# A fused decoder block on one core: reciprocal halves behind the copy of P, and the second weights ahead of the residual

## The chip, the core and the metric

The kernel runs on one core of one Trainium2 chip. The metric is the device time of one execution in microseconds (us). A run of the kernel gives one such time; the median of three runs is compared.

## What is computed

The program takes 4096 tokens of 512 features (16 sequences of 256) and runs four stages over them. Cut to what matters here:

```python
x = layernorm(x + mamba_and_gated_mlp(x))               # stages 1 and 2, untouched by the change
# stage 3, attention: 16 heads of 32, over 256 context tokens per sequence
q, k, v = x @ Wq.T + bq, ctx @ Wk.T + bk, ctx @ Wv.T + bv
p = softmax(q k^T / sqrt(32))                            # per head
x = layernorm(x + (p v) @ Wo.T + bo)
# stage 4, quantised MLP: 512 -> 2048 -> 512, the second product in 8 bits
h  = relu(x @ w1.T + b1);  hq = fp8(h);  wq = fp8(w2)
x  = layernorm(x + fp16(hq @ wq.T + b2))
```

## The kernel before

The tokens are cut into 8 tiles of 512 (NP = 8), that is two sequences each. Every stage is one function that writes five queues, one per engine, and a stage runs all 8 tiles before the next begins: tile 0 and tile 7 are written out, tiles 1 to 6 are a hardware loop (`steps`, line 60). The order of work on each engine is the order in which the code issues it; engines meet only at semaphores (`wait_ge`). Products in 32 bits are made from three products of rounded parts, high and low (`mm3`, lines 75 to 77), so each operand needs a "high" copy by ACT and a "low" rest by DVE or POOL.

**Attention** (`stage_attention`). A tile is 8 steps, n = 0 to 7; a step is four heads of one sequence. In step n the names stand for this:

- `scores(i, n + 1)` (L1701, PE): the scores of the next step into four banks SC.
- `row_max` (L1567, DVE): the negative maximum of each row, before ACT's exponentials (`exp`, L1417), which also leave the row sums in `sums`.
- `turn_p` (L1710, PE): four transposes of one head's P into the single bank PT; `take_pT` (L1573, DVE) copies PT to `at_pT`. There is one PT bank, so each `turn_p` waits for the copy before it (`pte`).
- `values` (L1722, PE): P times V for the step before, which needs all four copies of that step.
- `project(i, slot, half)` (L75 to L77, PE): two half projections for each of 16 slots, put between these as filling. Their results go alternately to banks AB[0] (even slots) and AB[1] (odd slots); DVE takes them in `take` (L1543, L1547 or L1553), which counts `pout`.
- `invert(i, g)`, at odd n, when the four heads' sums of both sequences are there: DVE's reciprocal (L1578), then its high half (the CAST, L1580) and its low half (L1582) into `at_r_hl`. `turn_r` (L1730, PE) transposes these into AB[1] at the next even n, ACT copies them (`take_rT`, L1423), `spread` (L1735) broadcasts them, and `normalise` (L1587, DVE) scales the heads' output.
- `statistics` (L1557) and `gather` (L1563), DVE: the layer norm's statistics of the tile before, in steps 3, 4 and 5. POOL then makes the reciprocal root (L889, L891) and normalises (L1498), SP stores the tile (L1366), and loads the next residual into the same tile of memory, to which POOL adds the bias (L1521). POOL also makes the low halves of the context (L1346) and of the heads' output (L1503).

DVE's queue in an odd step n of the loop:

```python
take_pT(i, n, 0); take_pT(i, n, 1)
split_u(i + 1, ...)                 # n = 1 and 3
statistics / gather                 # n = 3, (4), 5
invert(i, n // 2)
take_pT(i, n, 2)
take(i, 2 * n + 1)
row_max(i, n + 1, 0) ...
```

**Quantised MLP** (`stage_quantised_mlp`). Per tile PE makes 16 chunks of the hidden layer (`chunk`, 12 matmuls each), ACT turns each into 8 bits (`relu`, L1970), and then PE makes four groups of 16 matmuls with the 8-bit second weights `w2q` (L2071). The first 7 chunks of tile 0 are made in the last attention tile. The weights come through 8 staging tiles `qm_stage`: 16 pieces of w1, then 16 pieces of w2 (256 KB each), each of which waits for its staging tile's last user. ACT rounds each w2 piece to 8 bits (L214) between its relus of tile 0. SP's single queue issues all of it, in the order of the code: 8 pieces of w2, the store of attention's last tile (L1366), the tokens of tile 1 (L1933), the residual of tile 0 (L1937), 8 more pieces of w2.

## Time and profile before

| | us |
|---|---|
| median of 3 runs (lowest, highest) | 2758.64 (2756.23, 2761.95) |
| the profiled execution, its own time | 2757.51 |
| its span, first to last instruction | 2755.7 |
| PE busy | 2675.0 (97%) |
| DVE busy | 1530.9 (56%) |
| ACT busy | 1021.6 (37%) |
| POOL busy | 670.6 (24%) |

The span is what the trace covers; 1.8 us of the execution lie outside it. In the span the mixer ends at about 780 us, the gated MLP at about 1590, attention runs from about 1592 to 2285, the quantised MLP from there to the end. A middle tile of attention takes 84.43 us, the distance between two equal instructions of neighbouring tiles (a transposition at 1783.27 us and its like at 1867.70).

### The profile page before, as it was taken

The page shows a single profiled execution, that of the slowest core. Times are in us where ns is not written, and L with a number is a line of the kernel's source. Part 1 is how long each engine was busy: PE and PEld are TensorE (multiplying, and loading weights), DVE is VectorE, ACT ScalarE, POOL GpSimd, SP SyncE. Part 2 cuts the span into 40 slices and gives each one's busy share as a digit, 9 for nine tenths or more (in the row PEclk, how much of TensorE's full clock was granted, in tenths as well). Part 3 has the DMA queues.
Part 4 walks back from the last instruction along what each step waited for, and adds up shares of the span by engine and source line. Part 5 has one row for each costly group of instructions (what it writes and reads, how often), then busy time and mean ns, then how long its engine had stood idle before and what let it go on. Part 6 is the DMA issues. An engine that isn't in the chain of part 4 may idle for free.

```text
span 2755.7 us, 42318 instructions
## 1 busy us (share of the span) xinstructions
PE 2675.0 (97%) x15264; PEld 2074.0 (75%) x15264; DVE 1530.9 (56%) x2561; ACT 1021.6 (37%) x2375; POOL 670.6 (24%) x594
## 2 busy tenths in 40 slices
PE   7999999999999999999999989999999998999999
PEld 5777777777778888888888867777777766777776
DVE  8797797788785331333133377777777773111122
ACT  6334334434434222122212255555555553222221
POOL 5553453463361100010001101332223321000000
PEclk9999999999999999999999999999999999999999
DMA  4101101101114101110112030111011123211111
GB/s 152 46 2 46 46 0 46 46 0 46 46 47 139 62 19 42 61 61 14 47 61 96 23 108 11 60 61 39 30 61 53 57 93 114 83 48 46 46 46 46
DMA packets 85482, 147.83 MB, mean 54 GB/s; under 512 B 4032, under 2 KB 17984, under 8 KB 85408
## 3 DMA queue, kind: packets, MB, share of 16 engines
q1 hardware_dynamic: 85408, 146.84, 15.3%
q8 instruction: 46, 0.75, 0.1%
q14 instruction: 28, 0.23, 0.0%
HBM read 113.27 MB, written 33.55 MB: 53 GB/s over the span
## 4 chain that ended last, share of the span: by engine, by line
PE 87%; DVE 8%; issue 2%; ACT 1%; DMA 1%; POOL 0%; DVEq 0%; SPq 0%; POOLq 0%; ACTq 0%
PE ps L75 22%; PE ps L77 22%; PE ps L76 22%; PE ps L1710 4%; PE ps L2071 4%; PE ps L780 3%; PE ps L1722 2%; DVE mx_cv L585 1%; PE ps L1701 1%; PE ps L756 1%; DVE at_pT L1573 1%; DVE mx_m L593 1%; PE ps L768 1%; PE ps L1730 1%; DVE at_r_hl L1580 1%
## 5 line engine op out<-in xcount | busy, mean ns | idle before, releaser
L1417 ACT ACTIVATE at_pr<-ps,at_nm 128x256 f32<-128x256 f32 x512 | 235.9, 473 | 191.7 <-DVE at_nm L1567 191.7
L1110 DVE TENSOR_TENSOR gm_m_lo<-gm_m,gm_m_hi 128x512 fp32r<-128x512 f32 (+1 forms) x88 | 61.0, 693 | 416.8 <-ACT gm_m_hi L1027 416.8
L75 PE MATMUL ps<-sh_u_hi,gm_gu_hi 128*128 128x512 f32 (+1 forms) x704 | 274.7, 390 | 1.6 <-DVE gm_gu_lo L227 1.6
L76 PE MATMUL ps<-sh_u_lo,gm_gu_hi 128*128 128x512 f32 (+1 forms) x704 | 274.6, 390 | 0.0
L77 PE MATMUL ps<-sh_u_hi,gm_gu_lo 128*128 128x512 f32 (+1 forms) x704 | 274.6, 390 | 0.0
L1573 DVE COPY at_pT<-ps 128x512 f32<-128x512 f32 x256 | 176.1, 688 | 127.4 <-PE ps L1710 124.1
L1021 ACT ACTIVATE gm_sg<-ps 128x512 f32<-128x512 f32 (+1 forms) x88 | 52.7, 598 | 518.4 <-PE ps L77 518.3
L75 PE MATMUL ps<-sh_u_hi,qm_w_hi 128*128 128x512 f32 x512 | 201.4, 393 | 0.0
L77 PE MATMUL ps<-sh_u_hi,qm_w_lo 128*128 128x512 f32 x512 | 199.4, 390 | 0.0
L76 PE MATMUL ps<-sh_u_lo,qm_w_hi 128*128 128x512 f32 x512 | 199.3, 389 | 0.0
L530 POOL TENSOR_TENSOR mx_m<-mx_m,mx_g 128x512 f32<-128x512 f32 x128 | 185.0, 1445 | 45.6 <-DVE mx_m L595 45.3
L585 DVE SCALAR_TENSOR_TENSOR mx_cv<-ps,mx_cols,mx_cv 128x510 f32<-128x510 f32 (+2 forms) x240 | 176.2, 742 | 23.3 <-ACT mx_cv L427 16.7
L1710 PE MATMUL ps<-sh_ident,at_pr 128*128 128x128 f32 x1024 | 160.8, 280 | 28.3 <-DVE at_pT L1573 26.6
L1970 ACT ACTIVATE qm_h<-ps,qm_cols 128x512 fp8e4<-128x512 f32 x121 | 83.1, 687 | 262.0 <-PE ps L77 262.0
L1710 PEld LDWEIGHTS ps<-sh_ident,at_pr 128*128 128x128 f32 x1024 | 117.3, 141 | 83.3 <-issue 25.9
L1567 DVE TENSOR_REDUCE at_nm<-ps 128x2 f32<-128x512 f32 x256 | 163.5, 680 | 0.2 <-PE ps L1701 0.2
L2002 DVE TENSOR_TENSOR sh_u_lo<-ps,sh_u_hi 128x512 fp32r<-128x512 f32 x28 | 19.2, 685 | 247.6 <-ACT sh_u_hi L1961 247.6
L593 DVE TENSOR_TENSOR_SCAN mx_m<-ps,mx_cols 128x512 f32<-128x512 f32 x128 | 155.0, 1211 | 0.0
L75 PEld LDWEIGHTS ps<-sh_u_hi,gm_gu_hi 128*128 128x128 f32 (+1 forms) x704 | 130.5, 185 | 31.2 <-issue 1.7
L76 PEld LDWEIGHTS ps<-sh_u_lo,gm_gu_hi 128*128 128x128 f32 (+1 forms) x704 | 130.5, 185 | 29.7
L77 PEld LDWEIGHTS ps<-sh_u_hi,gm_gu_lo 128*128 128x128 f32 (+1 forms) x704 | 130.5, 185 | 29.7
L75 PE MATMUL ps<-gm_dn_hi,gm_m_hi 128*128 128x512 f32 (+1 forms) x352 | 139.3, 396 | 0.8
(252 smaller groups left out, 6331.1 us busy)
## 6 DMA issues: line engine op xcount, KB each, us to landing
sh_xf<-x_scratch SPq DMA_DIRECT2D x16, 1024.0 KB, 7.5
mx_xr<-in_x SPq DMA_DIRECT2D x8, 1024.0 KB, 5.9
h_scratch<-mx_xr SPq DMA_DIRECT2D x8, 1024.0 KB, 5.0
sh_xf<-h_scratch SPq DMA_DIRECT2D x8, 1024.0 KB, 8.2
gm_xr<-in_x SPq DMA_DIRECT2D x8, 1024.0 KB, 7.3
gm_r<-h_scratch SPq DMA_DIRECT2D x8, 1024.0 KB, 6.1
x_scratch<-gm_r SPq DMA_DIRECT2D x8, 1024.0 KB, 5.1
at_cf<-in_ctxT SPq DMA_DIRECT2D x16, 512.0 KB, 3.7
```

The source lines that it names most:

```text
L75: nc.tensor.matmul(out, l_hi, r_hi, start=first, stop=False)
L76: nc.tensor.matmul(out, l_hi, r_lo, start=False, stop=False)
L77: return nc.tensor.matmul(out, l_lo, r_hi, start=False, stop=last)
L530: G(m0[h % 4][:, :], m0[h % 4][:, :], g0[:, :], ALU.mult).then_inc(s["M"], 1)
L585: V.scalar_tensor_tensor(dst[:, :, back:SEQ], src[:, :, 0:SEQ - back], conv_w[:, c, 3 - back:4 - back], dst[:, :, back:SEQ], ALU.mult, ALU ...
L593: V.tensor_tensor_scan(m0[h % 4][:, :], bank[:, :], eye0[:, :], 0.0, ALU.mult, ALU.add)
L1417: A(pr[h][:, t, :], SC[h][:, SEQ * t:SEQ * t + SEQ], ACT.Exp, bias=nm[:, 4 * n + h, t:t + 1], accum_out=sums[:, 2 * b + t, 4 * g + h:4 * g ...
L1567: V.tensor_reduce(nm[:, 4 * n + h, :], SC[h][:, :].rearrange("p (t k) -> p t k", t=2), AX.X, ALU.max, negate=True).then_inc(s["nm"], 1)
L1573: V.tensor_copy(pT[:, h, :, :].rearrange("p b q -> p (b q)"), PT[:, :]).then_inc(s["pte"], 1)
L1710: last = T.transpose(PT[:, SEQ * kb + P * t:SEQ * kb + P * t + P], pr[h][:, t, P * kb:P * kb + P], ident[:, :])
L1970: A(h8[:, c, :], HB[c % 3][:, :], ACT.Relu, bias=b1[:, c:c + 1], saturate=False).then_inc(s["h8"], 1)
L2071: last = T.matmul(YB[t][:, :], h8[:, c, P * t:P * t + P], w2q[:, c, :], start=(c == 0), stop=(c == KF - 1))
```

## The change

1. Attention, DVE: `invert` keeps only the reciprocal. The two halves are a new function, `halves`, called after the third copy of P. The statistics and the gathering of steps 3, 4 and 5 go behind that copy, behind the halves, and behind `take(i, 2n + 1)`.
2. Attention, PE: at even n, `turn_r` goes from ahead of the projection's first half to between its halves; so do the waits on `pout` and, in the last tile, on the hidden chunks of the next stage.
3. Quantised stage, SP: tile 1's tokens are loaded ahead of the store of attention's last tile (`load_tokens`), and the residual of tile 0 behind the last 8 pieces of w2.
4. Quantised stage, PE: in every tile the second product begins when 14 of 16 chunks are rounded, and waits for the last two in front of the 15th matmul. Before, only the last tile did so.

```diff
--- before.py
+++ after.py
@@ -1391,7 +1391,9 @@
         sp.wait_ge(prev.s["st"], 16 * NP)
         steps(sp, main)
 
+        sp.wait_ge(s["st"], 16 * (NP - 1))
         me.nxt.wt.load(sp, 24)
+        me.nxt.load_tokens(sp, 0)
         store(NP - 1)
 
     def scalar(act):
@@ -1573,9 +1575,13 @@
             V.tensor_copy(pT[:, h, :, :].rearrange("p b q -> p (b q)"), PT[:, :]).then_inc(s["pte"], 1)
 
         def invert(i, g):
-            hi, lo = slice(4 * g, 4 * g + 4), slice(AH + 4 * g, AH + 4 * g + 4)
+            hi = slice(4 * g, 4 * g + 4)
             dve.wait_ge(s["e"], 8 * QS * i + 16 * (g + 1))
             V.reciprocal(rinv[:, :, hi], sums[:, :, hi]).then_inc(s["rinv"], 1)
+
+        def halves(i, g):
+
+            hi, lo = slice(4 * g, 4 * g + 4), slice(AH + 4 * g, AH + 4 * g + 4)
             dve.wait_ge(s["rinv"], HG * i + g + 1)
             V.tensor_copy(r_hl[:, :, hi], rinv[:, :, hi]).then_inc(s["rhi"], 1)
             dve.wait_ge(s["rhi"], HG * i + g + 1)
@@ -1609,6 +1615,13 @@
                     normalise(i, n // 2 - 1)
                 elif n in TURN:
                     split_u(i + 1, TURN[n][1])
+                if n % 2 == 1:
+                    invert(i, n // 2)
+                take_pT(i, n, 2)
+                if n % 2 == 1:
+                    halves(i, n // 2)
+                if has(i, 2 * n + 1, more):
+                    take(i, 2 * n + 1)
                 if not step_0(i):
                     if n == 3:
                         statistics(i - 1, 0, before(i, 5) + 1)
@@ -1618,11 +1631,6 @@
                     elif n == 5:
                         statistics(i - 1, 3, before(i, 8) + 1)
                         gather(i - 1)
-                if n % 2 == 1:
-                    invert(i, n // 2)
-                take_pT(i, n, 2)
-                if has(i, 2 * n + 1, more):
-                    take(i, 2 * n + 1)
                 if not more and n == 2:
                     me.nxt.constants(dve)
                 elif not more and n > 3:
@@ -1741,16 +1749,7 @@
                     turn_p(i, n - 1, 3)
                 elif not step_0(i):
                     turn_p(i - 1, QS - 1, 3)
-
-                if ahead(i, 2 * n) and n % 2 == 0:
-                    pe.wait_ge(me.nxt.s["h8"], ahead(i, 2 * n))
-                if n == 0 and not step_0(i):
-                    pe.wait_ge(s["pout"], before(i, 0))
-                    turn_r(i - 1, HG - 1)
-                elif n % 2 == 0 and n > 0:
-                    pe.wait_ge(s["pout"], before(i, 2 * n, more))
-                    turn_r(i, n // 2 - 1)
-                elif n in TURN:
+                if n in TURN:
                     pe.wait_ge(s["pout"], before(i, 2 * n))
                     turn(i + 1, TURN[n][0])
                 if has(i, 2 * n, more):
@@ -1762,11 +1761,23 @@
                     elif n in (3, 5, 7):
                         pe.wait_ge(s["on"], HG * i + n // 2)
                     project(i, 2 * n, 0)
-                    project(i, 2 * n, 1)
                 elif ahead(i, 2 * n) is not None:
                     if n % 2 == 1:
                         pe.wait_ge(s["on"], HG * i + n // 2)
-                    me.nxt.chunk(pe, 0, ahead(i, 2 * n), bank(i, 2 * n))
+                    me.nxt.chunk(pe, 0, ahead(i, 2 * n), bank(i, 2 * n), 0)
+
+                if n == 0 and not step_0(i):
+                    pe.wait_ge(s["pout"], before(i, 0))
+                    turn_r(i - 1, HG - 1)
+                elif n % 2 == 0 and n > 0:
+                    if ahead(i, 2 * n):
+                        pe.wait_ge(me.nxt.s["h8"], ahead(i, 2 * n))
+                    pe.wait_ge(s["pout"], before(i, 2 * n, more))
+                    turn_r(i, n // 2 - 1)
+                if has(i, 2 * n, more):
+                    project(i, 2 * n, 1)
+                elif ahead(i, 2 * n) is not None:
+                    me.nxt.chunk(pe, 0, ahead(i, 2 * n), bank(i, 2 * n), 1)
                 if n > 0:
                     values(i, n - 1)
                 elif not step_0(i):
@@ -1896,6 +1907,11 @@
     def load_small(sp):
         sp.dma_start(cols[:, :], inp["qm_cols"]).then_inc(su.small, 16)
 
+    def load_tokens(sp, i):
+
+        sp.wait_ge(s["T"], KD * (i + B) + KD)
+        sp.dma_start(xf[:, :, :], tokens(x2)[i + 1]).then_inc(s["xf"], 16)
+
     def constants(dve):
         dve.wait_ge(su.small, smalls)
         nc.vector.tensor_copy(b2h[:, :], b2).then_inc(su.dve, 1)
@@ -1918,24 +1934,22 @@
         act.wait_ge(s["h"], KF * i + c + 1)
         nc.scalar.activation(h8[:, c, :], bank[:, :], ACT.Relu, bias=b1[:, c:c + 1], saturate=False).then_inc(s["h8"], 1)
 
-    me.load_small, me.constants, me.chunk, me.relu = load_small, constants, chunk, relu
+    me.load_small, me.constants, me.chunk, me.relu, me.load_tokens = load_small, constants, chunk, relu, load_tokens
 
     def sync(sp):
         xs, os = tokens(x2), tokens(out)
 
         def main(i):
             at(sp, s["st"], 16 * i)
-            if not step_0(i):
+            if step_0(i):
+                wt.load(sp, len(pieces))
+
+                sp.wait_ge(prev.s["proj"], prev.projected)
+            else:
                 sp.wait_ge(prev.s["st"], 16 * NP)
-                sp.dma_start(r[:, :, :], xs[i]).then_inc(s["xr"], 16)
-            if not final(i):
-                sp.wait_ge(s["T"], KD * (i + B) + KD)
-                sp.dma_start(xf[:, :, :], xs[i + 1]).then_inc(s["xf"], 16)
-            if step_0(i):
-
-                sp.wait_ge(prev.s["proj"], prev.projected)
-                sp.dma_start(r[:, :, :], xs[i]).then_inc(s["xr"], 16)
-                wt.load(sp, len(pieces))
+            sp.dma_start(r[:, :, :], xs[i]).then_inc(s["xr"], 16)
+            if not step_0(i) and not final(i):
+                load_tokens(sp, i)
             for t in range(TT) if final(i) else ():
                 sp.wait_ge(s["ln"], TT * i + t + 1)
                 sp.dma_start(os[i][:, t, :], r[:, t, :]).then_inc(s["st"], 16)
@@ -1943,8 +1957,6 @@
                 sp.wait_ge(s["ln"], TT * i + TT)
                 sp.dma_start(os[i], r[:, :, :]).then_inc(s["st"], 16)
 
-
-        sp.wait_ge(prev.s["st"], 16 * (NP - 1))
         steps(sp, main)
 
         sp.wait_ge(s["st"], 16 * (NP - 1) + 16 * TT)
@@ -2037,8 +2049,9 @@
 
     def tensor(pe):
         T = nc.tensor
-        h8_count = pe.alloc_register("qm_h8_count")
-        pe.reg_mov(h8_count, 2 * KF)
+        most, all_of = pe.alloc_register("qm_h8_most"), pe.alloc_register("qm_h8_all")
+        pe.reg_mov(most, 2 * KF - 2)
+        pe.reg_mov(all_of, 2 * KF)
 
         def turn(i, k):
             if k == 0:
@@ -2060,14 +2073,11 @@
                 pe.wait_ge(*wt.highs())
 
                 pe.wait_ge(prev.s["bn"], TT * NP)
-            if final(i):
-                pe.wait_ge(s["h8"], KF * i + KF - 2)
-            else:
-                wait_count(pe, s["h8"], KF * i + KF, h8_count, KF)
+            wait_count(pe, s["h8"], KF * i + KF - 2, most, KF)
             for t in range(TT):
                 for c in range(KF):
-                    if final(i) and t == 0 and c >= KF - 2:
-                        pe.wait_ge(s["h8"], KF * i + c + 1)
+                    if t == 0 and c == KF - 2:
+                        wait_count(pe, s["h8"], KF * i + KF, all_of, KF)
                     last = T.matmul(YB[t][:, :], h8[:, c, P * t:P * t + P], w2q[:, c, :], start=(c == 0),
                                     stop=(c == KF - 1))
                 last.then_inc(s["y"], 1)
```

DVE, step 5 of a middle tile, from the second copy of P to the last row maxima, first before (its REGISTER_ALU rows only advance a count):

```order
L1557 BN_STATS at_stats<-at_r 128x6 [waits at_pout]
L1563 BN_AGGR at_mv<-at_stats 128x2 [waits at_bn,at_pout] x4
L1577 REGISTER_ALU
L1578 RECIPROCAL at_rinv<-at_sums 128x4x4 [waits at_e]
L1579 REGISTER_ALU
L1580 CAST at_r_hl<-at_rinv 128x4x4 [waits at_rinv]
L1582 TENSOR_TENSOR at_r_hl<-at_rinv,at_r_hl 128x4x4 [waits at_rhi]
L1571 REGISTER_ALU
L1573 COPY at_pT<-ps 128x512 [waits at_pv,at_pt]
L1546 REGISTER_ALU
L1547 SCALAR_TENSOR_TENSOR at_q_lo<-ps,at_cols,at_q_hi 128x512 [waits at_phi]
```

The same place with the change:

```order
L1580 RECIPROCAL at_rinv<-at_sums 128x4x4 [waits at_e]
L1573 REGISTER_ALU
L1575 COPY at_pT<-ps 128x512 [waits at_pv,at_pt]
L1585 REGISTER_ALU
L1586 CAST at_r_hl<-at_rinv 128x4x4 [waits at_rinv]
L1588 TENSOR_TENSOR at_r_hl<-at_rinv,at_r_hl 128x4x4 [waits at_rhi]
L1548 REGISTER_ALU
L1549 SCALAR_TENSOR_TENSOR at_q_lo<-ps,at_cols,at_q_hi 128x512 [waits at_phi]
L1559 BN_STATS at_stats<-at_r 128x6 [waits at_pout]
L1565 BN_AGGR at_mv<-at_stats 128x2 [waits at_bn,at_pout] x4
L1568 REGISTER_ALU
L1569 TENSOR_REDUCE at_nm<-ps 128x2 [waits at_S] x2
```

The third copy stood behind one statistics instruction, four gathers, the reciprocal and both halves; now only the reciprocal is ahead of it, and the rest stands ahead of the row maxima of step 6.

PE, the start of step 0 of a middle tile, before (the last transposition of P, the transposition of the halves, then a projection of slot 0):

```order
L1710 MATMUL ps<-sh_ident,at_pr_195 128x128 [waits at_pte]
L1710 MATMUL ps<-sh_ident,at_pr_195 128x128 x3
L1748 ISA
L1728 ISA [waits at_pout]
L1730 MATMUL ps<-sh_ident,at_r_hl 32x128 [waits at_rlo]
L1730 MATMUL ps<-sh_ident,at_r_hl 32x128 x3
L1668 REGISTER_ALU
L75 MATMUL ps<-at_wv_hi,at_c_hi 128x512 [waits at_pout]
L76 MATMUL ps<-at_wv_lo,at_c_hi 128x512
L77 MATMUL ps<-at_wv_hi,at_c_lo 128x512
L75 MATMUL ps<-at_wv_hi,at_c_hi 128x512
L76 MATMUL ps<-at_wv_lo,at_c_hi 128x512
```

and with the change, from the projection on:

```order
L75 MATMUL ps<-at_wv_hi,at_c_hi 128x512 [waits at_pout]
L76 MATMUL ps<-at_wv_lo,at_c_hi 128x512
L77 MATMUL ps<-at_wv_hi,at_c_lo 128x512
L75 MATMUL ps<-at_wv_hi,at_c_hi 128x512
L76 MATMUL ps<-at_wv_lo,at_c_hi 128x512
L77 MATMUL ps<-at_wv_hi,at_c_lo 128x512
L1770 REGISTER_ALU
L1736 ISA [waits at_pout]
L1738 MATMUL ps<-sh_ident,at_r_hl 32x128 [waits at_rlo]
L1738 MATMUL ps<-sh_ident,at_r_hl 32x128 x3
L75 MATMUL ps<-at_wv_hi,at_c_hi 128x512
```

The transposition of the halves with its waits on `at_pout` and `at_rlo` went behind six matmuls of the projection.

SP, from the store of attention's last tile in the program before:

```order
L1366 DMA x_scratch<-at_r 128x4x512 [waits at_ln]
L1933 DMA sh_xf<-x_scratch 128x4x512 [waits sh_T,at_st]
L1937 DMA qm_r<-x_scratch 128x4x512 [waits at_proj]
L204 DMA qm_stage_228<-in_w2T 128x512 [waits set_hi]
L204 DMA qm_stage_229<-in_w2T 128x512 [waits set_hi]
L204 DMA qm_stage_230<-in_w2T 128x512 [waits set_hi]
L204 DMA qm_stage_231<-in_w2T 128x512 [waits set_hi]
```

and with the change:

```order
L1913 DMA sh_xf<-x_scratch 128x4x512 [waits sh_T]
L1366 DMA x_scratch<-at_r 128x4x512 [waits at_ln]
L204 DMA qm_stage_228<-in_w2T 128x512 [waits set_hi]
L204 DMA qm_stage_229<-in_w2T 128x512 [waits set_hi]
L204 DMA qm_stage_230<-in_w2T 128x512 [waits set_hi]
L204 DMA qm_stage_231<-in_w2T 128x512 [waits set_hi]
L204 DMA qm_stage_232<-in_w2T 128x512 [waits set_hi]
```

The load of `sh_xf` went ahead of the store, that of `qm_r` behind the eight pieces, so that the pieces follow the store at once.

## Rows read from the trace of the kernel before

**Rows 1.** The page, part 1: busy time, share of the span, instructions

```profile
PE 2675.0 (97%) x15264; PEld 2074.0 (75%) x15264; DVE 1530.9 (56%) x2561; ACT 1021.6 (37%) x2375; POOL 670.6 (24%) x594
```

**Rows 2.** Waits of PE, 1700 to 2200 us: total, times, longest

```profile
PE ps L1710 <- DVE at_pT L1573: 15.6, 23, 1.0
```

**Rows 3.** Timeline, PE, step 1: start, us, instruction, idle before and releaser

```profile
1866.19 0.60 PE L1710 MATMUL ps<-sh_ident,at_pr 128*128 128x128 f32 x4
...
1868.45 0.66 PE L1710 MATMUL ps<-sh_ident,at_pr 128*128 128x128 f32 x4 [0.75 <-DVE at_pT L1573]
...
1872.42 1.07 PE L1722 MATMUL ps<-at_pT,at_v 128*32 128x256 f32 x16
```

**Rows 4.** Timeline, DVE, the same step: the third copy of P

```profile
1867.70 0.69 DVE L1573 COPY at_pT<-ps 128x512 f32<-128x512 f32 x1
```

**Rows 5.** Timeline, PE, step 2 (no stall) and the end of step 4

```profile
1877.36 0.60 PE L1710 MATMUL ps<-sh_ident,at_pr 128*128 128x128 f32 x4
...
1878.80 0.66 PE L1710 MATMUL ps<-sh_ident,at_pr 128*128 128x128 f32 x4
...
1898.97 0.60 PE L1710 MATMUL ps<-sh_ident,at_pr 128*128 128x128 f32 x4
...
1900.68 0.65 PE L1710 MATMUL ps<-sh_ident,at_pr 128*128 128x128 f32 x4 [0.20 <-DVE at_pT L1573]
...
1904.01 1.07 PE L1722 MATMUL ps<-at_pT,at_v 128*32 128x256 f32 x16
```

**Rows 6.** Timeline, PE, step 5 into step 6

```profile
1908.72 0.60 PE L1710 MATMUL ps<-sh_ident,at_pr 128*128 128x128 f32 x4
...
1911.26 0.66 PE L1710 MATMUL ps<-sh_ident,at_pr 128*128 128x128 f32 x4 [1.02 <-DVE at_pT L1573]
...
1915.28 1.07 PE L1722 MATMUL ps<-at_pT,at_v 128*32 128x256 f32 x16
...
1918.16 0.60 PE L1710 MATMUL ps<-sh_ident,at_pr 128*128 128x128 f32 x4
```

**Rows 7.** Timeline, POOL, step 5

```profile
1909.00 1.28 POOL L1503 TENSOR_TENSOR at_o_lo<-at_o,at_o_hi 128x512 fp32r<-128x512 f32 x1
```

**Rows 8.** Timeline, DVE, step 5: CAST, row maxima; step 6: first copy

```profile
1909.32 0.99 DVE L1580 CAST at_r_hl<-at_rinv 128x16 fp32r<-128x16 f32 x1
...
1911.78 1.28 DVE L1567 TENSOR_REDUCE at_nm<-ps 128x2 f32<-128x512 f32 x2
...
1916.98 0.69 DVE L1573 COPY at_pT<-ps 128x512 f32<-128x512 f32 x1
```

**Rows 9.** Timeline, ACT, step 6: the high half of a projection

```profile
1915.39 0.69 ACT L1410 ACTIVATE at_k_hi<-ps,at_cols 128x512 fp32r<-128x512 f32 x1 [0.51 <-PE ps L77]
```

**Rows 10.** Timeline, step 7: tile 0's low half and bias adds; a middle tile's adds

```profile
1676.01 1.16 DVE L1582 TENSOR_TENSOR at_r_hl<-at_rinv,at_r_hl 128x16 fp32r<-128x16 f32 x1
...
1675.86 5.00 POOL L1521 TENSOR_TENSOR at_r<-at_r,at_cols 128x512 f32<-128x512 f32 x4
...
1930.17 5.01 POOL L1521 TENSOR_TENSOR at_r<-at_r,at_cols 128x512 f32<-128x512 f32 x4 [0.66 <-DMA at_r<-x_scratch]
```

**Rows 11.** Chain that ended last, 2299 to 2331 us: start, us, what

```profile
2299.65 9.78 DMA qm_stage<-in_w2T
...
2314.24 0.62 ACT qm_w2q L214
...
2315.58 5.21 PE ps L2071 x16
```

**Rows 12.** Stretches: engines' busy us (instructions), PEclk, DMA share, GB/s

```profile
2304.00:2308.30 4.30, 4.29 (x21) 3.34 (x20) 0.00 (x0) 0.00 (x0) 0.00 (x0) 1.00 1.05 405
2312.00:2314.00 2.00, 0.00 (x0) 0.00 (x0) 0.00 (x0) 2.00 (x5) 0.00 (x0) 0.50 0.48 184
```

**Rows 13.** Waits of PE, 2200 us to the end: total, times, longest

```profile
PE ps L2071 <- ACT qm_h L1970: 10.9, 7, 7.3
```

**Rows 14.** Timeline, PE, tile 1 of the quantised stage: its first product group

```profile
2377.06 3.61 PE L2071 MATMUL ps<-qm_w2q,qm_h 128*128 128x512 fp8e4 x16 [0.60 <-ACT qm_h L1970]
```

## The prediction

> **What bounds the kernel now.** I read the page first: PE is busy for 2675.0 us of a span of 2755.7, 97% [rows 1]. So nothing that only frees another engine can help, and all that the change can win lies in PE's 80 us of idle time or at a low clock. Next, PE's waits in the middle of attention: nearly all of its idle time there is one kind, the fourth transposition of P waiting for DVE's third copy, 15.6 us in 23 waits over 500 us [rows 2]. That is 5.9 tiles of 84.43 us, so four waits and 2.6 us in a tile. They stand in steps 1, 3, 4 and 5. In the quantised stage PE waits 10.9 us for ACT, 7.3 of them at once in tile 0 and 3.6 in six tiles [rows 13]. The change touches just these two places, and the question is how much of each wait really goes, and what is late next.
>
> **The third copy in steps 1 and 3.** I count from the start of a step's third transposition. Where nothing stalls, the fourth follows after 1.44 us (1877.36 to 1878.80) [rows 5]; in step 1 after 2.26 (1866.19 to 1868.45) [rows 3], so 0.82 us is lost. PE goes on 0.75 after the copy starts (1867.70 to 1868.45) [rows 3, 4], so a copy that starts by 0.69 costs nothing. With both halves behind it, the reciprocal alone is ahead, and it is done before that. The whole 0.82 goes. Step 3 loses as much now, by a statistics instruction and shorter halves; both go behind, again 0.82.
>
> Next, the transposition of the halves behind half a projection. From the fourth transposition to the values it takes 3.97 us in step 1 (1868.45 to 1872.42) [rows 3] and 3.33 in step 4, where no halves are transposed [rows 5]. Four such transpositions cost about 0.4, so 0.24 is waiting: `turn_r` writes bank AB[1] and waits for the take of the slot before, which DVE begins only behind the third copy. Behind six matmuls that wait is covered. I take 0.24 at each of the four places and keep 0 and 0.3 as bounds. Steps 1 and 3 thus give 1.05 us each, step 7, which has no stall of the first kind, 0.24.
>
> **Steps 4 and 5, where the moved work is due next.** DVE's total does not shrink; the statistics and halves now stand ahead of the next step's row maxima. A vector instruction of this size takes some 0.64 (two row maxima, 1.28) [rows 8]. In step 4, the fourth transposition follows the third by 1.71 us (1898.97 to 1900.68) [rows 5], so 0.27 is lost. Two statistics, 1.2 us, move behind a copy that could start only 0.3 earlier, so the row maxima begin 0.9 later than now, and so does the fourth copy, for which the values wait 3.33 us after the fourth transposition. I get the values at 5.03, where they are now at 5.04 (1904.01 less 1898.97) [rows 5]. Step 4 gives nothing.
>
> Step 5 stalls most: 2.54 against 1.44 (1908.72 to 1911.26) [rows 6], so 1.10 can go, and 0.27 with the other wait. But the CAST is held by POOL: it starts at 1909.32 and ends at 1910.31, just after POOL's low half ends at 1910.28 [rows 7, 8]. It will wait there still, and ACT's later exponentials push POOL's work back by about 0.4. From the third transposition: copy 0.7, CAST done at 1.6 to 2.0, low half and take 0.8, statistics 0.6, gathers 0.3: the row maxima begin at 3.4 to 3.8, against 3.06 now [rows 6, 8], while PE is 1.1 ahead of now. Behind them hangs a chain: exponentials, the copy of the halves, a high half by ACT, the take, the first copy of step 6. It is 5.20 long now (1911.78 to 1916.98) with 0.6 to 0.8 of waiting for PE in it [rows 8, 9], so about 4.4 when it binds. PE's second transposition of step 6 then starts at 3.8 + 4.4 + 0.75 = 8.95, against 9.44 now (1918.16) [rows 6] and 8.0 if nothing held it. Step 5 gives 0.5; its bounds are 0 and 1.4.
>
> A middle tile: 1.05 + 1.05 + 0 + 0.5 + 0.24 = 2.85 us, six of them 17.1. Tiles 0 and 7 have other neighbours (no statistics, or weights to round), and tile 0 collides in step 7: POOL adds the bias from 1675.86 on for 5.00 us, and the halves come in the middle of it [rows 10]. For both I take half a middle tile, 1.4 each, between nothing and 2.85. Attention: 19.9 us.
>
> **The second weights.** In tile 0 the product starts at 2315.58 [rows 11], but PE had stood still for 7.3 us then, since 2308.3 [rows 13]. It waits for ACT's last rounding (2314.24 and 0.62), and that for the pieces of w2: the first of the last eight was issued at 2299.65 and landed 9.78 us later [rows 11], behind a store and two loads of 1 MB each. The queue moves 405 GB/s at that time [rows 12], so the two loads cost 2 x 1.05 MB / 405 GB/s = 5.2 us. One is now issued before the store, in a stretch in which the queue is nearly empty, and one behind the pieces. The pieces are also issued 1.7 earlier, of use only if the queue has room. So the last piece is rounded at 2309.4 or up to 0.6 sooner; the last two relus no longer stand in the way, since the product begins at 14. It starts at 2309.3: 6.3 us won, bounds 5 and 7.3. The residual lands 2.6 behind the last piece, near 2311.3, and DVE needs it for the split of tile 1's tokens by 2312: just in time.
>
> **The clock.** In the hole the granted clock falls: 0.50 of 2.4 GHz, that is 1.2 GHz, from 2312 to 2314, after PE had stood idle for 4 us [rows 12]. The first product group took 5.21 us [rows 11], in tile 1 the same takes 3.61 [rows 14]. With an idle stretch of 1.2 us ending at 2309.3 I expect full clock and 1.6 us back; if it falls all the same, nothing.
>
> **Product at 14.** In the six middle tiles PE idles 0.60 us each before the product for the last relu [rows 13, 14]; fourteen matmuls last 3 us, so all goes: 3.6 us. The last tile had it already. The register waits add nothing that shows.
>
> **The sum.** 19.9 + 6.3 + 1.6 + 3.6 = 31.4 us. The profiled execution took 2757.5, so 2726.1; the median of three stands 1.1 above it, so **2727** us, 1.1% less. A difference under 0.2%, some 5.5 us, a measurement of this kernel can't tell from no change.
>
> **The rivals.**
> - *Row maxima late everywhere.* If the chain behind them binds in steps 1 and 3 too, attention gives half, 10 us: 2737. For it: DVE carries the same work, and step 3's row maxima begin at 2.9, close to where they hold PE. Against: in step 1 they begin 0.4 earlier than now. Chance 0.22.
> - *Step 7 meets POOL's bias adds.* The halves come at about 1930.9 now, and POOL's run is at 1930.17 to 1935.2 in a middle tile; in tile 0 a low half beside it took 1.16 us [rows 10]. Both halves can wait for one add each, 1.25 us; the row maxima of the next tile come 1.9 later, and 0.24 won turns to 0.6 lost: 0.85 in six tiles, 5 us: 2732. Against: the gathers are 2 us later, and with them POOL's root, normalisation, the store, the load and so the run. Chance 0.08. The Trainium skill (SBUF — State Buffer, Who interferes with whom) states the rule behind it: VectorE and GpSimd share a port pair, a cast or an instruction with two SBUF inputs needs it, and who comes first holds it for the whole instruction. The trace agrees with the 1.16 and the 0.99 above.
> - *Everything goes*, in steps 4 and 5 too: 0.27 + 1.37 instead of 0.5 in a middle tile, 7 us more: 2719. Chance 0.10.
> - *The hole stays in part.* The pieces come no sooner (a store that holds the queue), 4 us less and the low clock again: 2733. Chance 0.05.
> - *Slower.* Every pair of halves finds POOL busy twice, in steps 1, 3, 5 and 7. Each pair then takes 2.5 us more ahead of the row maxima; beyond the slack of some 0.7 in steps 1 and 3, PE loses 0.85 there against now, as much in step 5, 1.6 in step 7: 4.1 us a tile, 33 in eight, less 11.5 from the quantised stage: 2779. It decides from 1.5 us lost a tile. Against it: POOL runs one instruction at the CAST of step 5 [rows 7, 8], and in steps 1 and 3 its one instruction ends while the copy runs. Chance 0.03.
> - *No change*: attention trades all it wins and the hole closes by half: 2753. Chance 0.03.
>
> The forecast keeps 0.49, from 2721 to 2734 by its own bounds. For 8 in 10 the range takes in the first two rivals and the third: **2719 to 2741**. Faster by over 0.2%: 0.94; within: 0.03; slower: 0.03.
>
> **What would show it.** A middle tile of 81.6 us instead of 84.43. Fourth transpositions 1.44 after the third in all steps; a new wait of PE in step 4 at the values, and in step 6 at the second transposition, both on DVE's copy. The CAST of step 1 short, that of step 5 ending with POOL. The eight pieces behind the store, the product of tile 0 at about 31 us minus attention's 20 before its place now, its first group at 3.6 and a clock of 1.00. No wait of the product for ACT in tiles 1 to 6. I am wrong if the fourth transposition still waits, if the row maxima's delay costs more than it saves, or if the first group stays at 5.2.

## The result, and the profile after

The changed kernel takes **2726.26 us** in the median (2725.51 to 2733.49, 4 runs) against 2759.02 for the kernel before on the same chip: a ratio of 0.9885, with a 95% interval of 0.9874 to 0.9897. The forecast was 2727, in a range of 2719 to 2741.

The profiled execution of the change took 2733.49, the longest of its four. It loses those 7 us ahead of step 2 of attention's first tile, nearly all of them in code that the change doesn't touch, as a second trace of it shows below. So I read both traces from one place on. A **mark** is the start of `spread`'s matmul, of which each tile has four, in steps 2, 4, 6 and in step 0 of the next tile (L1735 before, L1743 now). The first mark of attention stands at 1625.85 us before and at 1633.14 after; from there to the end of the span it is 2755.7 - 1625.85 = 1129.85 us before and 2731.7 - 1633.14 = 1098.56 after: **31.3 us less**, where the sum said 31.4.

| us, after less before | forecast | measured |
|---|---|---|
| a middle tile (distance of equal marks 84.43, now 81.80) | -2.85 | -2.63 |
| of it steps 1 and 3 (marks of step 0 to 2, 2 to 4) | -1.05 each | -0.99, -0.97 |
| of it steps 4 and 5 together (4 to 6) | -0.5 | -0.5 |
| of it step 7 (marks of step 6 to 0) | -0.24 | -0.18 |
| tile 0; tile 7 | -1.4; -1.4 | -2.66; -0.07 |
| attention, first to last mark | -19.9 | -18.5 |
| last mark to the product of tile 0 | -6.3 | -6.6 |
| first product group | -1.6 | -1.6 |
| product at 14, six tiles | -3.6 | -4.6 |

The page of the changed kernel, part 1, answers to [rows 1]. PE's busy time is what it was; the span of this execution is 2731.7, so what went is its idle time.

```profile
PE 2673.9 (98%) x15264; PEld 2074.9 (76%) x15264; DVE 1520.9 (56%) x2561; ACT 1020.7 (37%) x2375; POOL 671.0 (25%) x594
```

The waits of PE from 1700 to 2200 us, against [rows 2]. The 15.6 us for the third copy are gone; in their place stand 3.4 us of a kind that was not there, the values (L1730) waiting for the fourth copy, twice a tile.

```profile
PE ps L1730 <- DVE at_pT L1575: 3.4, 12, 0.4
```

The timeline of PE in the changed kernel: step 1, then step 4, then step 5 into step 6 of a middle tile (start, duration, instruction, idle before and releaser).

```profile
1865.56 0.60 PE L1718 MATMUL ps<-sh_ident,at_pr 128*128 128x128 f32 x4
1867.01 0.66 PE L1718 MATMUL ps<-sh_ident,at_pr 128*128 128x128 f32 x4
...
1870.80 1.07 PE L1730 MATMUL ps<-at_pT,at_v 128*32 128x256 f32 x16
...
1896.39 0.60 PE L1718 MATMUL ps<-sh_ident,at_pr 128*128 128x128 f32 x4
...
1901.41 1.07 PE L1730 MATMUL ps<-at_pT,at_v 128*32 128x256 f32 x16 [0.16 <-DVE at_pT L1575]
...
1906.11 0.60 PE L1718 MATMUL ps<-sh_ident,at_pr 128*128 128x128 f32 x4
...
1907.55 0.66 PE L1718 MATMUL ps<-sh_ident,at_pr 128*128 128x128 f32 x4
...
1911.85 1.07 PE L1730 MATMUL ps<-at_pT,at_v 128*32 128x256 f32 x16 [0.42 <-DVE at_pT L1575]
...
1915.03 0.66 PE L1718 MATMUL ps<-sh_ident,at_pr 128*128 128x128 f32 x4
```

In step 1 the fourth transposition follows the third by 1.45 us instead of 2.26 [rows 3], and nothing waits. In step 4 the values come 5.02 after the third transposition, where they came 5.04 after it [rows 5]. In step 5 the fourth transposition is 1.44 behind the third instead of 2.54, but the second transposition of step 6 comes 8.92 behind the third, against 9.44 [rows 6]. The wait that the profile lists there stands ahead of that transposition, at the values: 0.42 for the fourth copy.

DVE and POOL in step 5 of the changed kernel:

```profile
1907.35 0.86 DVE L1586 CAST at_r_hl<-at_rinv 128x16 fp32r<-128x16 f32 x1
...
1909.91 1.29 DVE L1569 TENSOR_REDUCE at_nm<-ps 128x2 f32<-128x512 f32 x2
```

```profile
1906.89 1.29 POOL L1505 TENSOR_TENSOR at_o_lo<-at_o,at_o_hi 128x512 fp32r<-128x512 f32 x1
```

The CAST ends at 1908.21, POOL's instruction at 1908.18, as it was in [rows 7, 8]. The row maxima begin 3.80 after the third transposition, against 3.06 before.

Step 7 of tile 0, against [rows 10]: POOL's bias adds begin at 1679.99 and take 4.99 us, and both halves fall into them.

```profile
1681.48 1.06 DVE L1586 CAST at_r_hl<-at_rinv 128x16 fp32r<-128x16 f32 x1
1682.57 1.21 DVE L1588 TENSOR_TENSOR at_r_hl<-at_rinv,at_r_hl 128x16 fp32r<-128x16 f32 x1
```

```profile
1684.58 0.61 PE L1738 MATMUL ps<-sh_ident,at_r_hl 128*32 128x128 f32 x4 [0.86 <-DVE at_q_lo L1549]
```

The waits of PE from 2200 us to the end, against [rows 13]. Of 10.9 us for ACT's relus and weights 0.7 are left. New are two waits of the hidden chunks in tile 7, 1.1 and 1.0.

```profile
PE ps L1718 <- DVE at_pT L1575: 1.5, 2, 0.9
PE ps L75 <- issue: 1.1, 1, 1.1
PE ps L75 <- DVE qm_w_lo L225: 1.0, 1, 1.0
PE ps L1718 <- ACT at_pr L1419: 0.9, 1, 0.9
PE ps L2081 <- ACT qm_w2q L214: 0.7, 1, 0.7
```

DVE in tile 7 of the changed kernel, where PE stands still from 2224.71 to 2225.82. The profile names no releaser for this wait; the first low half of a hidden chunk's weights ends at 2225.71, just before PE goes on. It is behind two statistics, which stood ahead of the third copy before; PE arrives earlier than it did, and DVE's queue is no shorter.

```profile
2223.24 0.69 DVE L1575 COPY at_pT<-ps 128x512 f32<-128x512 f32 x1 [0.21 <-PE ps L1718]
2223.85 1.28 DVE L1559 BATCH_NORM_STATS2 at_stats<-at_r 128x6 f32<-128x512 f32 x2
2225.04 1.28 DVE L225 TENSOR_TENSOR qm_w_lo<-qm_stage,qm_w_hi 128x512 fp32r<-128x512 f32 x2
```

The chain that ended last, 2290 to 2306 us, against [rows 11], and the clock at the end of the hole (columns as in [rows 12]):

```profile
2290.85 5.66 DMA qm_stage<-in_w2T
...
2296.53 1.25 ACT qm_w2q L214 x2
...
2297.82 3.63 PE ps L2081 x16
```

```profile
2296.50:2298.50 2.00, 1.30 (x9) 0.69 (x8) 0.00 (x0) 1.97 (x4) 0.00 (x0) 1.00 1.03 402
```

PE idles 0.70 us there instead of 7.29, the granted clock stays at 1.00 (2.4 GHz), and the first group takes 3.63 instead of 5.21. In tile 1 of the quantised stage the first group has no wait ahead of it, against [rows 14]:

```profile
2356.96 3.62 PE L2081 MATMUL ps<-qm_w2q,qm_h 128*128 128x512 fp8e4 x16
```

### The profile page after: what moved, and what is told of

It reads as the page before. It is cut to its first block, busy times and chain, and to the rows that moved or that the text cites. A ratio compares the mean times of both kernels' runs of the same rounds, so it can differ in the third digit from the quotient of the medians.

```text
span 2731.7 us, 42325 instructions
## 1 busy us (share of the span) xinstructions
PE 2673.9 (98%) x15264; PEld 2074.9 (76%) x15264; DVE 1520.9 (56%) x2561; ACT 1020.7 (37%) x2375; POOL 671.0 (25%) x594
## 4 chain that ended last, share of the span: by engine, by line
PE 89%; DVE 7%; issue 2%; ACT 1%; DMA 1%; POOL 0%; DVEq 0%; SPq 0%; POOLq 0%; ACTq 0%
PE ps L75 23%; PE ps L77 22%; PE ps L76 22%; PE ps L1718 4%; PE ps L2081 4%; PE ps L780 3%; PE ps L1730 2%; PE ps L1709 2%; DVE mx_cv L585 1%; DVE mx_m L593 1%; PE ps L756 1%; PE ps L768 1%; PE ps L717 1%; PE ps L806 1%; PE ps L1662 1%
## 5 line engine op out<-in xcount | busy, mean ns | idle before, releaser
L75 PEld LDWEIGHTS ps<-sh_u_hi,gm_gu_hi 128*128 128x128 f32 (+1 forms) x704 | 130.9, 186 | 31.3 <-issue 1.7
```

The source lines that it names most:

```text
L75: nc.tensor.matmul(out, l_hi, r_hi, start=first, stop=False)
```

## The experiments

Ten kernels ran, one of them the change once more. Each is held against the kernel before on its own chip (medians 2756.85 to 2761.7) and, trace to trace, by the marks. "Mark to end" is the time from the first mark to the end of the span: 1129.85 before, 1098.56 for the change.

### One part of the change at a time

*Attention alone.* Parts 1 and 2 of the change on the kernel before; SP's order and the quantised stage stay as they were.

```diff
+                if n % 2 == 1:
+                    invert(i, n // 2)
+                take_pT(i, n, 2)
+                if n % 2 == 1:
+                    halves(i, n // 2)
...
```

> The attention half of the change alone; the quantised stage and SP's order as before. If the parts add up, attention gives what the trace of the change shows between equal marks: 2.6 us in each of six middle tiles, 2.7 in tile 0, nothing in tile 7, 18.4 us in all: a ratio to the kernel before of 0.9933, some 2740.5 us. Rival: the two halves help one another (an earlier end of attention meets the loads of the weights differently), then this gives under 15 or over 22 us.

2739.45 us, ratio 0.994 (0.9923 to 0.9957); mark to end 1111.93, 17.9 less. Its marks agree with those of the change step for step within 0.03.

*SP's order alone.* Part 3.

```diff
+        sp.wait_ge(s["st"], 16 * (NP - 1))
         me.nxt.wt.load(sp, 24)
+        me.nxt.load_tokens(sp, 0)
...
```

> SP's new order alone: tile 1's tokens ahead of the last store, the residual behind the second weights; the product still waits for 16 rounded chunks. Theory (the two loads cost 5.2 us of queue): the product of tile 0 starts about 6 us sooner and its first group takes 3.6 us instead of 5.2, 7.5 us in all: 2751.5 us. Rival (the clock falls all the same after the rest of the hole): 6 us: 2753.

2750.18, ratio 0.9973 (0.9962 to 0.9983); mark to end 1122.47, 7.4 less. The product of tile 0 waits 1.37 us, now for the last relu.

*Product at 14 alone.* Part 4.

```diff
+            wait_count(pe, s["h8"], KF * i + KF - 2, most, KF)
...
+                    if t == 0 and c == KF - 2:
+                        wait_count(pe, s["h8"], KF * i + KF, all_of, KF)
```

> Only the product begun at 14 of 16 chunks, in every tile. Theory: the 0.60 us wait goes in six tiles, and what a first group takes more than the others (3.61 against 3.45) with it: 0.76 a tile, 4.6 us; tile 0 keeps its hole, since the last weights are late there: 2754.5 us. Rival: the wait alone, 3.6 us: 2755.4; nothing in tile 0 by either.

2752.59, ratio 0.998 (0.997 to 0.9989); mark to end 1123.19, 6.7 less, 0.9 of it in attention's first tile, which it doesn't touch (there the clock falls at another moment than in the trace of before; see tiles 0 and 7 below). The hole of tile 0 is 6.32 us instead of 7.29. Its expectation had nothing in tile 0: PE now waits for the last weights alone, and no longer for the last relu behind them. The low clock at its end stays (first group 4.99).

The three medians stand 18.3, 7.6 and 5.2 below before, 31.1 together; the change stands 32.8 below. The parts add up within what the runs can tell. In the hole of tile 0 two of them overlap a little: 5.9 us for SP's order, 1.0 for the product at 14, 6.6 for both.

### What the order of DVE is worth without that of PE

*Halves transposed first.* The changed kernel with PE's order of before in attention.

```diff
+                if n == 0 and not step_0(i):
+                    pe.wait_ge(s["pout"], before(i, 0))
+                    turn_r(i - 1, HG - 1)
...
                     project(i, 2 * n, 0)
+                    project(i, 2 * n, 1)
...
-                if n == 0 and not step_0(i):
-                    pe.wait_ge(s["pout"], before(i, 0))
-                    turn_r(i - 1, HG - 1)
...
-                if has(i, 2 * n, more):
-                    project(i, 2 * n, 1)
```

> The changed kernel with TensorE's order of before in attention: the halves are transposed ahead of the first half projection again; VectorE keeps the new order. By the prediction's term alone (a wait of 0.24 at each of four places that the half projection covers) this costs 0.24 x 4 in each of eight tiles, 7 us: 2733. Theory now: it costs more, since the take that the transposition waits for stands behind the halves, and TensorE comes to it 0.8 earlier than before: the wait grows to 0.24 + 0.8 in steps 1 and 3 and to some 0.5 in steps 5 and 7, together 2.5 to 3 us a tile, so that the order of VectorE alone gives attention next to nothing: 2745 to 2750. If it costs nothing, 2726, the move was no part of the gain.

2739.52, ratio 0.9934 (0.9918 to 0.9951): 13.4 us slower than the change, between the 7 and the 19 to 24 of the two expectations. A middle tile takes 83.46, 1.67 more than the change's: 0.40 and 0.48 for steps 1 and 3, 0.3 for steps 4 and 5, 0.48 for step 7. PE's waits from 1700 to 2200 us:

```profile
PE ps L1738 <- DVE at_q_lo L1549: 7.9, 12, 1.0
PE ps L1738 <- DVE at_r L1555: 2.1, 6, 0.4
PE ps L1738 <- DVE at_v L1545: 1.6, 6, 0.3
PE ps L1730 <- DVE at_pT L1575: 1.0, 6, 0.2
```

The first three are the transposition of the halves (L1738) waiting for the take behind which its bank comes free. So VectorE's order alone gives 0.97 us a tile and the small move on TensorE 1.67. The forecast had it the other way, 0.24 a place: it read that wait where PE came late, and took the number over to a kernel in which PE comes earlier.

### Why steps 4 and 5 gave less than they could

*Statistics ahead again.* The changed kernel, but statistics and gathers back ahead of the third copy; the halves stay behind it.

```diff
-                if n % 2 == 1:
-                    invert(i, n // 2)
-                take_pT(i, n, 2)
-                if n % 2 == 1:
-                    halves(i, n // 2)
-                if has(i, 2 * n + 1, more):
-                    take(i, 2 * n + 1)
                 if not step_0(i):
...
                         gather(i - 1)
+                if n % 2 == 1:
+                    invert(i, n // 2)
+                take_pT(i, n, 2)
+                if n % 2 == 1:
+                    halves(i, n // 2)
...
```

> The whole change, but the statistics and the gathering stay where they were, ahead of the reciprocal and the third copy; the two halves stay behind it. Theory (the row maxima of steps 5 and 6 are late because of the moved statistics, and the chain behind them binds): step 3 loses 0.24 by one statistics instruction ahead of the copy, step 4 is as before, but step 5 gives 1.37 instead of 0.5, so a middle tile takes 81.1 to 81.3 us instead of 81.8, and the last tile's loss of 1.4 us goes: 4 to 5 us faster than the change, 2722. Rival (the CAST held by POOL in step 5 is what delays the row maxima, the statistics matter little): no faster than the change or up to 2 us slower, 2726 to 2728, step 5 still at 0.5.

By its trace the theory is right in a middle tile: 81.03 us, steps 4 and 5 gain 1.32 instead of 0.50, mark to end 1093.93, 4.6 less than the change. In tile 7 it isn't: steps 4 and 5 lose 0.20 against before instead of 1.39, but step 7 loses 1.03, since the low half (1.21 us) and a subtraction (1.78) meet POOL's bias adds there, and the tile as a whole is where it was. By its timed runs no gain over the change is shown: 2728.91 in the median, ratio 0.9895 (0.9878 to 0.9911), where the change has 0.9885 and the theory's 4 to 5 us would be 0.987. The profiled execution alone took 2725.98. I can't say what the other three lost, since they have no trace.

*Statistics in DVE's idle time.* One statistics instruction in each of steps 3 to 6, between the first and the second copy, where DVE waits 1.1 us for PE.

```diff
                 take_pT(i, n, 0)
+                if not step_0(i) and 3 <= n <= 6:
+                    statistics(i - 1, n - 3, before(i, n + 2) + 1)
+                    if n == 6:
+                        gather(i - 1)
                 take_pT(i, n, 1)
...
-                if not step_0(i):
-                    if n == 3:
-                        statistics(i - 1, 0, before(i, 5) + 1)
...
```

> The changed kernel with the residual's statistics taken out of the place behind the third copy: one of the four in each of steps 3 to 6, between the first and the second copy of P, where VectorE stands idle 1.1 us for TensorE's next transposition; the gathers behind the last, in step 6. Theory (what is still lost in steps 4 and 5 is lost because the statistics stand ahead of the next step's row maxima): nothing is late now, steps 4 and 5 gain 1.3 to 1.6 against before instead of 0.5, a middle tile takes 80.7 to 81.0, and the 1.39 us that tile 7 lost against before (low half of the second weights behind the statistics) mostly goes. 2717 to 2721. Rival (what is left there is VectorE's total or GpSimd's CAST, and the place of the statistics doesn't matter, as the timed runs of d_statistics_ahead suggest): 81.6 to 81.9 a tile, 2725 to 2728.

2723.72, ratio 0.9876 (0.986 to 0.9893), mark to end 1096.04. The middle tile is 80.73, steps 4 and 5 gain 1.58, and from 1700 to 2200 us PE has no wait left at all. So what the change left there was the statistics ahead of the row maxima, and nothing else. But tile 7 lost 0.8 against the change, and the product began 37.14 us after the last mark instead of 34.17. PE and ACT at the end of tile 7:

```profile
2253.26 0.76 PE L1738 MATMUL ps<-at_rT,at_sel 128*128 128x512 f32 x1 [2.73 <-ACT at_rT L1425]
```

```profile
2251.34 1.29 ACT L214 ACTIVATE qm_w_hi<-qm_stage 128x512 fp32r<-128x512 f32 x2 [9.10 <-DMA qm_stage<-in_w1T]
2252.54 0.57 ACT L1425 ACTIVATE at_rT<-ps 32x512 fp32r<-32x512 f32 x1
```

ACT's copy of the transposed halves stands in the queue behind a rounding, that one behind a load of weights, that load behind the store of the tile before on SP's queue, the store behind POOL's normalisation, and that behind the gathers, which are now a step later. The product's later begin is not another wait: the granted clock falls to 0.50 within the 2.73 us and stays there until about 2259.4 (columns as in [rows 12]), and PE's work of that time takes 3.0 us longer.

```profile
2253.00:2259.00 6.00, 5.75 (x14) 4.52 (x15) 3.65 (x3) 1.22 (x3) 4.15 (x4) 0.50 0.75 215
```

*The same, with the gathers in step 5.*

```diff
                 take_pT(i, n, 0)
+                if not step_0(i) and n in (3, 4, 5):
+                    t = {3: 0, 4: 1, 5: 3}[n]
+                    statistics(i - 1, t, before(i, 5 + t) + 1)
+                    if n == 5:
+                        gather(i - 1)
                 take_pT(i, n, 1)
...
+                if not step_0(i) and n == 4:
+                    statistics(i - 1, 2, before(i, 7) + 1)
                 if n % 2 == 1:
                     invert(i, n // 2)
...
-                if not step_0(i):
...
```

> As e_statistics_idle, but the gathers in step 5 instead of step 6: statistics 0 in step 3 and 1 in step 4 between the first and the second copy of P, statistics 2 in step 4 ahead of the third copy (0.77 us of idle time there), statistics 3 and the gathers in step 5 between the first and the second copy. Theory: e_statistics_idle lost its gain in tile 7 because its gathers came a step later, so the residual's store came some 4 us later against the end of the tile (2240.28 with the last mark at 2253.26, in g_after_again 2239.81 and 2256.93), the loads of weights behind it on SP's queue with it, and ACT stood 9.1 us waiting for a piece while the copy that TensorE needed queued behind that (2.73 us idle); and the product of tile 0 began 37.1 us after the last mark instead of 34.2. With the gathers in step 5 the store comes earlier than in the changed kernel: middle tile 80.7 to 80.9, the 2.73 gone, the product again 34.2 after the last mark. 2715 to 2719. Rival (the low halves of the second weights bound tile 7 whatever stands where, or the third copy of step 4 is late again by the statistics ahead of it): 2720 to 2724.

2723.1, ratio 0.9881 (0.9865 to 0.9898), mark to end 1093.75. The 2.73 are gone and the low clock behind them, the product is back at 34.20 after the last mark, the middle tile is 80.74. The forecast of 2715 to 2719 was missed all the same: tile 7 has a new wait of 1.72, for a reason that neither theory named. DVE and POOL there:

```profile
2241.18 1.05 DVE L1586 CAST at_r_hl<-at_rinv 128x16 fp32r<-128x16 f32 x1
2242.26 1.22 DVE L1588 TENSOR_TENSOR at_r_hl<-at_rinv,at_r_hl 128x16 fp32r<-128x16 f32 x1
2243.40 2.44 DVE L225 TENSOR_TENSOR qm_w_lo<-qm_stage,qm_w_hi 128x512 fp32r<-128x512 f32 x2
```

```profile
2239.69 5.00 POOL L1523 TENSOR_TENSOR at_r<-at_r,at_cols 128x512 f32<-128x512 f32 x4
```

The earlier store brings the residual earlier, and with it POOL's bias adds, to the very place of the halves: this is the collision that the forecast held as a rival for step 7.

*The adds behind the halves.* The kernel just shown, with two waits on POOL, in tile 0 and in tile 7.

```diff
             pool.wait_ge(s["xr"], 16 * i + 16)
+            if step_0(i):
+                pool.wait_ge(s["rlo"], HG * i + HG)
+            elif final(i):
+                pool.wait_ge(*me.nxt.wt.lows(7))
```

> k_statistics_by_5 with two waits added on GpSimd: in tile 0 its four bias adds wait for the low half of step 7's reciprocals, in tile 7 for the low halves of the second weights' eighth piece (VectorE's two subtractions behind those halves). Theory (GpSimd's adds and VectorE's halves get in each other's way: in k_statistics_by_5 the adds ran from 2239.69 for 5.00 us, and the CAST in them took 1.05 us, the low half 1.22 and the two subtractions 2.44, against 0.17, 0.18 and 1.28 where GpSimd was idle; in tile 0 1.06 and 1.21): the durations fall back to 0.17, 0.18 and 1.28, the wait of 1.72 us in tile 7 (values, for VectorE's copy) and that of 0.85 in tile 0 (transposition of the halves) go, step 7 of tile 0 is 0.7 to 0.9 faster and the end of tile 7 1.5 to 1.8: 2.3 to 2.7 in all; lowest run 2718, median 2717.5 to 2721. Rival (the adds come too late for the next tile's residual, or for the last tile's, and the wait turns up there): no gain, 2720 to 2724, with a new wait behind the adds.

2720.28 (2716.84 to 2721.81), ratio 0.9853 (0.9836 to 0.9869), mark to end 1089.82. DVE and POOL in tile 7:

```profile
2244.20 0.16 DVE L1590 CAST at_r_hl<-at_rinv 128x16 fp32r<-128x16 f32 x1
2244.40 0.18 DVE L1592 TENSOR_TENSOR at_r_hl<-at_rinv,at_r_hl 128x16 fp32r<-128x16 f32 x1
2244.49 1.28 DVE L225 TENSOR_TENSOR qm_w_lo<-qm_stage,qm_w_hi 128x512 fp32r<-128x512 f32 x2
```

```profile
2245.92 5.01 POOL L1527 TENSOR_TENSOR at_r<-at_r,at_cols 128x512 f32<-128x512 f32 x4 [3.17 <-DVE qm_w_lo L225]
```

The theory is right: the durations are those it names, step 7 of tile 0 is 1.0 faster, both waits are gone, and nothing waits for the later adds. Tile 7 gained 2.9 where 1.5 to 1.8 were expected, and 3.9 is the whole by mark to end. 1.8 of the 2.9 is step 7, with the collision; the other 1.1 isn't the adds'. In the trace of the kernel without the two waits, and not in this one, the granted clock fell in step 4 of tile 7, from 2209 to about 2212:

```profile
2210.00:2211.00 1.00, 1.00 (x9) 0.99 (x6) 1.00 (x3) 0.00 (x0) 0.00 (x0) 0.50 0.00 0
```

So the two waits on POOL are worth 2.8, close to the 2.3 to 2.7 expected. The Trainium skill (SBUF — State Buffer, Who interferes with whom) has the rule: a VectorE cast can run in a mode that uses the port pair shared with GpSimd, and a VectorE instruction with two SBUF inputs contends for it with a GpSimd instruction that reads SBUF; who comes first holds the pair for the whole instruction. By that rule, the traces agree: 1.05 and 1.22 against 0.16 and 0.18. This version has the lowest median of the study, 8.7 us below the change by mark to end and 6.0 by the medians; the intervals of the two ratios don't meet.

### The second weights and the clock

*Residual ahead of the pieces.* The changed kernel, with tile 0's residual ahead of the last eight pieces again; the tokens stay early.

```diff
             if step_0(i):
-                wt.load(sp, len(pieces))
-
                 sp.wait_ge(prev.s["proj"], prev.projected)
             else:
                 sp.wait_ge(prev.s["st"], 16 * NP)
             sp.dma_start(r[:, :, :], xs[i]).then_inc(s["xr"], 16)
+            if step_0(i):
+                wt.load(sp, len(pieces))
```

> The changed kernel with the quantised stage's first residual ahead of the last eight pieces of its weights again; the tokens stay early. Theory (each 1 MB load ahead of the pieces costs its own time on the queue, 2.6 us at 405 GB/s): the last piece lands 2.6 later, the product of tile 0 starts 2.0 to 2.6 later than in the changed kernel, having waited 2.7 to 3.3 instead of 0.7; its idle stretch is then close to that at whose end the clock fell in before. With full clock 2728.5, with half clock in the first group 2730. Rival (the early tokens are what matters, the residual shares the queue's engines with the pieces without delaying them): product in the same place, 2726.

2730.52, ratio 0.991 (0.9893 to 0.9926), mark to end 1102.79. PE's product, and the clock behind the hole:

```profile
2292.43 5.31 PE L2081 MATMUL ps<-qm_w2q,qm_h 128*128 128x512 fp8e4 x16 [3.47 <-ACT qm_w2q L214]
```

```profile
2294.00:2296.00 2.00, 2.00 (x7) 0.68 (x5) 0.26 (x1) 0.00 (x0) 0.00 (x0) 0.50 0.00 0
```

The product starts 36.93 after the last mark instead of 34.17, 2.76 later for one load of 1 MB: the 2.6 of the forecast's sum. It cost 4.2 by mark to end. Most of the rest is the clock: after 3.47 us of idle time the first group takes 5.31 at 0.50 (1.2 GHz), as it did after 7.29; after 1.37 (SP's order alone) and after 0.70 it takes 3.6.

### The change once more

The changed kernel, unaltered.

> The changed kernel itself, unaltered, so that the other three are held against it on the same chip, and so that it has a second trace. Time: 2726 again, within 2. In its first trace and in those of c_at_14_only and d_statistics_ahead the mixer's first mark of the stage stood 2.7 us later than in the traces of before, a_attention_only and b_sp_order_only, and attention began 4.4 to 7.3 later, in code that none of them changes. If that belongs to the program, the first mark is near 126.4 in this trace as well; if it is chance of one execution, it can as well be near 123.7. Middle tile 81.8 us either way.

2726.15, ratio 0.9894 (0.9877 to 0.991). Its second trace has the middle tile at 81.78 and mark to end at 1098.37, 0.2 from the first; the first mark stands at 1626.63, where it stood at 1633.14, and the instruction of the mixer that the expectation calls its first mark at 124.29, not near 126.4. So the 7 us belonged to that one execution, not to the program. Much of it is the clock. Against the second trace the first is some 2.3 us late from 50 us on; it falls back another 1.6 at 840 us and 3.0 at 1610, and at both places its granted clock is low where that of the second isn't:

```profile
839.00:843.00 4.00, 4.00 (x12) 3.09 (x11) 3.32 (x5) 0.50 (x2) 0.13 (x1) 0.57 0.01 4
1607.00:1614.00 7.00, 6.00 (x19) 4.96 (x19) 2.21 (x4) 3.59 (x16) 0.00 (x0) 0.52 0.00 0
```

## Why the prediction was right

**What bounds it.** Right. PE's busy time stayed within 1.1 us, and the 31 us are its idle time and some 3.2 us of low clock: the 1.6 that the forecast had, and 1.6 in tile 0 that it hadn't.

**Steps 1 and 3.** 0.99 and 0.97 for 1.05. The 0.82 went whole (1.45 between the transpositions). The other term, 0.24 behind half a projection, came out right only as a net: without the move of the transposition each place costs 0.3 to 0.5 in the new order, so the wait had to be covered for the 0.82 to count. As the price of that move, 0.96 a tile stood for 1.67.

**Steps 4 and 5.** The best of the working: values at 5.03 forecast, 5.02 measured; second transposition of step 6 at 8.95 forecast, 8.92 measured, and by the way forecast: row maxima at 3.80, 4.4 us from there to the first copy of step 6 (1909.91 to 1914.29), 0.74 more to PE. The reason given, row maxima behind the statistics, is shown by the kernel that puts these elsewhere: 1.58 instead of 0.50.

**Tiles 0 and 7.** Half a middle tile for both was a guess between its bounds, and each missed it on another side. Tile 0 gave 2.66, and 2.19 of it lie between its marks of steps 2 and 4, where the kernel before had a CAST held by POOL ahead of the third copy. The timelines of PE, DVE and POOL in that step before the change, and the clock behind it:

```profile
1637.72 0.63 PE L1710 MATMUL ps<-sh_ident,at_pr 128*128 128x128 f32 x4 [1.52 <-DVE at_pT L1573]
```

```profile
1635.78 0.99 DVE L1580 CAST at_r_hl<-at_rinv 128x16 fp32r<-128x16 f32 x1
```

```profile
1635.46 1.28 POOL L1346 TENSOR_TENSOR at_c_lo<-at_cf,at_c_hi 128x512 fp32r<-128x512 f32 x1 [0.92 <-ACT at_c_hi L1342]
```

```profile
1639.50:1643.00 3.50, 3.50 (x23) 2.13 (x24) 1.72 (x3) 3.50 (x15) 0.00 (x0) 0.51 1.01 336
```

That collision is still there (a CAST of 0.56 us), but the copy no longer stands behind it: PE waits 0.23 instead of 1.52, though 1.11 instead of 0.64 for the values behind it, and so begins these only 0.6 us sooner. The other 1.6 is the clock. Before, it stood at 0.51 from 1639.5 to 1643, right behind these waits; now it stays at 1.00 in that step. The fall is in the three traces with VectorE's old order in attention and in none of the nine with the new one. The working has no term for it, so this part of the gain is luck: without it attention would have given some 16.9 for 19.9. Tile 7 gave 0.07: its steps 0 to 3 gain 1.45, and its steps 4 and 5, which also carry low halves of the quantised stage's weights behind the statistics, lose 1.39. The two errors almost cancel: 2.7 for 2.8.

**The second weights and the clock.** 6.6 for 6.3 and 1.6 for 1.6. "Two loads of 1 MB are 5.2 us" is shown for one of them, 2.76; both together, with the earlier issue, brought the product 5.9 nearer.

**Product at 14.** This term is mis-sized, 4.6 for 3.6: it took the wait of 0.60 a tile and left out the gap of 0.16 within the first group, which goes with it; 0.76 x 6 = 4.6.

**The sum.** 31.3 for 31.4 is closer than the working was. Attention's terms came to 18.5 for 19.9, with 1.6 of unforeseen clock in them, and the product at 14 and the second weights made good 1.3 of that.

**The rivals.** *Row maxima late everywhere* didn't come: steps 1 and 3 kept their gain. It came in steps 4 and 5, as forecast. *Step 7 meets POOL's bias adds* came in the changed kernel for the halves of tile 0 alone, for 0.86; in a middle tile the halves are through at 1928.26 and the adds begin at 1930.04. *Everything goes* (2719) would have needed the statistics elsewhere; 2720.28 was reached that way, and with POOL's adds held back in two tiles. *Hole stays*, *slower* and *no change* have nothing for them in the trace.

What is still open: whether statistics ahead of the third copy are as good in timed runs as in their trace, why the clock falls in other places from one execution to the next, and where the first 2.3 us of difference come from.

## What to carry to other kernels

When a queue's work is reordered, look for the engine's idle time and put the movable instruction there, not just behind the one that hurts: the same four statistics cost TensorE 0.3 us a tile ahead of the third copy, 1.1 us a tile behind that copy, and nothing between two copies. Follow each moved instruction to the end of its chain, through stores, the loads queued behind them and what these release: a step later starved ACT of weights, a step earlier led POOL into DVE's way. And a wait read from a trace is a wait at that pace of the other engine: once PE came 0.8 us earlier, a place of 0.24 cost 0.3 to 0.5. Read the granted clock of every stretch that is compared, too: a stall can cost more behind it than in it.
